# A layer norm's scales: from a chain split between VectorE and GpSimd to a chain on GpSimd alone

## The reference, cut to what matters

```python
def _layernorm(x, axis=-1, eps=1e-05):
    m = jnp.mean(x, axis=axis, keepdims=True)
    v = jnp.var(x, axis=axis, keepdims=True)
    return (x - m) / jnp.sqrt(v + eps)

# x: (4, 1024, 256)
x = x + _layernorm(attn(_layernorm(x)))   # norm 1 inside, norm 2 outside
x = x + _layernorm(ffn(_layernorm(x)))    # norm 3 inside, norm 4 outside
```

## Time and profile before

| what | us |
|---|---|
| median of the 3 timed runs | 1262.3 |
| lowest and highest of them | 1260.84, 1262.65 |
| the profiled execution, its own time | 1258.12 |
| the profiled execution, its span | 1256.3 |
| busy in the span: PE, DVE, POOL, ACT | 1043.6, 705.6, 681.0, 625.3 |

### The profile page before, as it was taken

One profiled execution on the slowest core, in us unless ns is written; L12 is line 12 of the kernel. 1 busy time (PEld: TensorE's weight loads), 2 busy tenths in 40 slices (PEclk: granted clock), 3 DMA queues, 4 the chain that ended last, 5 costly groups with the idle time before them and its releaser, 6 DMA issues. The chain is left out here.

```text
span 1256.3 us, 15452 instructions
## 1 busy us (share of the span) xinstructions
PE 1043.6 (83%) x4736; PEld 832.8 (66%) x4736; DVE 705.6 (56%) x1280; ACT 625.3 (50%) x1190; POOL 681.0 (54%) x605
## 2 busy tenths in 40 slices
PE   4555578887867887797988899969999999999995
PEld 2122265664644655575777688859999999999884
DVE  1699998999988899976796442101111111111045
ACT  3784869778476586668554432212232222232234
POOL 2495967759469786578665347324343433332221
PEclk9676778898887897898999899979999999999998
DMA  5000010202002007113322589359998888887252
GB/s 180 18 28 6 34 34 18 68 1 83 2 1 84 1 18 227 42 22 110 83 96 67 172 236 208 55 150 347 337 316 266 264 276 251 262 273 227 41 176 101
DMA packets 140931, 162.68 MB, mean 129 GB/s; under 512 B 27976, under 2 KB 125984, under 8 KB 140832
## 3 DMA queue, kind: packets, MB, share of 16 engines
q1 hardware_dynamic: 124976, 142.70, 36.0%
q0 software_dynamic: 15872, 18.99, 7.7%
HBM read 135.20 MB, written 26.87 MB: 129 GB/s over the span
## 5 line engine op out<-in xcount | busy, mean ns | idle before, releaser
L1542 POOL TENSOR_TENSOR Ssum<-Ssum,S 128x512 f32<-128x512 f32 x240 | 301.5, 1270 | 105.9 <-DVE S L1162 104.7
L1014 PE MATMUL psum<-w,hT 128*128 128x256 f32 x1152 | 260.0, 384 | 4.2 <-issue 4.2
L1014 PEld LDWEIGHTS psum<-w,hT 128*128 128x128 f32 x1152 | 219.8, 193 | 34.4 <-issue 4.6
L1592 POOL DMA_INDIRECT acc_d<-y,ID x72 | 114.3, 1587 | 236.8 <-DMA acc_d<-y,ID 124.7
L1431 ACT ACTIVATE A<-dts,nea 128x512 f32<-128x512 f32 x256 | 177.3, 720 | 68.6 <-DVE S L1162 40.4
L1470 ACT ACTIVATE hT<-psum,bb 128x256 f32<-128x256 f32 x200 | 83.5, 470 | 244.7 <-PE psum L981 244.7
L981 PE MATMUL psum<-XT,w 128*128 128x256 f32 x800 | 182.8, 386 | 7.4 <-issue 6.5
L1138 DVE TENSOR_TENSOR psum<-us,psum 128x512 f32<-128x512 f32 x256 | 163.4, 682 | 31.6 <-PE psum L902 29.6
L981 PEld LDWEIGHTS psum<-XT,w 128*128 128x128 f32 x800 | 154.0, 194 | 33.9 <-issue 10.7
L1162 DVE TENSOR_TENSOR_SCAN S<-A,carry,psum 128x512 f32<-128x512 f32 x120 | 148.8, 1264 | 0.0
L1296 DVE TENSOR_TENSOR y<-bb,psum 128x256 f32<-128x256 f32 x72 | 27.0, 416 | 209.0 <-PE psum L1014 209.0
(11 more groups left out here) (149 smaller groups left out, 1314.3 us busy)
## 6 DMA issues: line engine op xcount, KB each, us to landing
w<-W SPq DMA_DIRECT2D x94, 1024.0 KB, 6.7
bb<-b SPq DMA_DIRECT2D x47, 128.0 KB, 7.8
xnb<-x SPq DMA_DIRECT2D x16, 256.0 KB, 3.0
Xr<-x SPq DMA_DIRECT2D x16, 256.0 KB, 4.6
x_d<-gb SPq DMA_DIRECT2D x8, 512.0 KB, 2.9
xn_d<-nb SPq DMA_DIRECT2D x8, 512.0 KB, 3.3
X<-x_d SPq DMA_DIRECT2D x16, 256.0 KB, 9.3
ACC<-acc_d SPq DMA_DIRECT2D x16, 256.0 KB, 5.9
```

Source lines behind the costliest of these rows:

```text
L1014: t = eng.matmul(bank(g)[:, 256 * k:256 * k + 256], hT[n % 2][:, f, 128 * k:128 * k + 128], w[:, f, :], start=f == 0, stop=f == 7)
L1542: eng.tensor_tensor(to, to, of, ALU.add).then_inc(nsum, 1)
L1592: eng.indirect_dma_start(acc_d, bass.IndirectOffsetOnAxis(ap=ID[:, col, 1:2].bitcast(u32), axis=0), y[n % NY][:, k, :], None, compute_op=A ...
```

## The change

The step `scales` leaves the plan. VectorE ends its part with the four `bn_aggr`. GpSimd does the rest in the step `stats`: it adds eps to the variance, negates the mean, raises to the power, and multiplies. `mv` gets two buffers per norm, since GpSimd now reads it, and the waits that guard `rs` and `nm` move from VectorE to GpSimd. The next `bn_stats` of VectorE carries a wait for its own last `bn_aggr` (`read`). The small extra chain for 8 edge rows at the start keeps its split.

```diff
@@ finishing
         if i:
             say("normal", 4, i - 1, False)
-        say("scales", 4, i)
@@ buffers
-        mv = {k: put(f"mv{k}", [128, 4, 2]) for k in (1, 2, 3, 4)}
+        mv = {k: [put(f"mv{k}{i}", [128, 4, 2]) for i in range(2)] for k in (1, 2, 3, 4)}
@@ VectorE
-            def scales(kind, i):
-                eng.wait_ge(rstd[kind], i + 1)
-                if i >= 2:
-                    eng.wait_ge(norma[kind], act_normals(kind, i - 2))
-                eng.scalar_tensor_tensor(nm[kind][i % 2], mv[kind][:, :, 0], -1.0, rs[kind][i % 2],
-                                         ALU.mult, ALU.mult).then_inc(nmd[kind], 1)
@@
+                        if j == 0 and read:
+                            eng.wait_ge(*read)
                         i = eng.bn_stats(stats[:, j, :], of(kind, b, j))
                     i.then_inc(statd[kind], 1)
-                    eng.wait_ge(statd[kind], 3 * b + 1)
+                    eng.wait_ge(statd[kind], 2 * b + 1)
+                    if b >= 2:
+                        eng.wait_ge(nmd[kind], b - 1)
                     for j in range(n):
-                        i = eng.bn_aggr(mv[kind][:, j, :], stats[:, j, :])
+                        i = eng.bn_aggr(mv[kind][b % 2][:, j, :], stats[:, j, :])
                     i.then_inc(statd[kind], 1)
-                    eng.wait_ge(statd[kind], 3 * b + 2)
-                    if b >= 2:
-                        eng.wait_ge(norma[kind], act_normals(kind, b - 2))
-                    eng.tensor_scalar(rs[kind][b % 2][:, 0:n], mv[kind][:, 0:n, 1], eps, None,
-                                      ALU.add).then_inc(statd[kind], 1)
+                    read = statd[kind], 2 * b + 2
@@ GpSimd
-                    eng.wait_ge(statd[kind], 3 * b + 3)
-                    eng.tensor_tensor(rs[kind][b % 2][:, 0:n], rs[kind][b % 2][:, 0:n], mhalf[:, 0:n],
-                                      ALU.pow).then_inc(rstd[kind], 1)
+                    r, m = rs[kind][b % 2], nm[kind][b % 2]
+                    eng.wait_ge(statd[kind], 2 * b + 2)
+                    if b >= 2:
+                        eng.wait_ge(norma[kind], act_normals(kind, b - 2))
+                    eng.tensor_scalar(r, mv[kind][b % 2][:, :, 1], 1e-5, None, ALU.add).then_inc(rstd[kind], 1)
+                    eng.tensor_scalar(m, mv[kind][b % 2][:, :, 0], -1.0, None, ALU.mult).then_inc(rstd[kind], 1)
+                    eng.wait_ge(rstd[kind], 3 * b + 1)
+                    eng.tensor_tensor(r, r, mhalf, ALU.pow).then_inc(rstd[kind], 1)
+                    eng.wait_ge(rstd[kind], 3 * b + 3)
+                    eng.tensor_tensor(m, m, r, ALU.mult).then_inc(nmd[kind], 1)
```

More of the change, by code:

```diff
@@ L1042, in apply @@
                                       nm[kind][i % 2][:, j:j + 1], ALU.mult, ALU.add).then_inc(normv[kind], 1)
+            read = None
             done = {}
@@ L1073, in _ @@
                         eng.wait_ge(edge_mv, 1)
-                        eng.bn_aggr(mv[4][0:8, 0, :], stats[0:8, 0, :]).then_inc(edge_mv, 1)
+                        eng.bn_aggr(mv[4][0][0:8, 0, :], stats[0:8, 0, :]).then_inc(edge_mv, 1)
                         eng.wait_ge(edge_mv, 2)
-                        eng.tensor_scalar(rs[4][0][0:8, 0:1], mv[4][0:8, 0, 1:2], eps[0:8], None,
+                        eng.tensor_scalar(rs[4][0][0:8, 0:1], mv[4][0][0:8, 0, 1:2], eps[0:8], None,
                                           ALU.add).then_inc(edge_mv, 1)
@@ L1107, in _ @@
                         eng.wait_ge(edge_mv, 4)
-                        eng.scalar_tensor_tensor(nm[4][0][0:8, 0:1], mv[4][0:8, 0, 0:1], -1.0, rs[4][0][0:8, 0:1],
+                        eng.scalar_tensor_tensor(nm[4][0][0:8, 0:1], mv[4][0][0:8, 0, 0:1], -1.0, rs[4][0][0:8, 0:1],
                                                  ALU.mult, ALU.mult).then_inc(edge_mv, 1)
@@ L1112, in _ @@
                                           ALU.mult, ALU.add).then_inc(edge_n, 1)
[L1113 to L1117, removed]
-                                eng.wait_ge(st_xn, 16 * b)
-                                eng.wait_ge(nT_out, 2 * b)
-                            apply(kind, b)
-                elif step == "scales":
-                    scales(*a)
+                    if both:
+                        if kind == 3:
+                            eng.wait_ge(st_xn, 16 * b)
+                            eng.wait_ge(nT_out, 2 * b)
+                        apply(kind, b)
                 elif step == "dt_sum":
@@ L1486, in _ @@
                     kind, b = a
-                    n = 4
                     if kind == 1 and b == 0:
```

## The result

| | before | changed |
|---|---|---|
| timed, median (range), us | 1262.47 (1260.84 to 1270.02) | 1250.91 (1250.09 to 1254.36) |
| ratio, 95% interval | 1 | 0.9903 (0.9882 to 0.9925) |
| profiled execution, us | 1258.12 | 1254.36 |
| its span, us | 1256.3 | 1252.6 |
| busy: VectorE / GpSimd, us | 705.6 / 681.0 | 684.6 / 704.9 |

The change makes the kernel 11.6 us faster. The forecast was 1246, with 1240 to 1252 as its own range: the sign holds, but of the 16.6 us of the forecast's sum five are missing, and the part of the sum that was to carry most of it is not the part that did.

What follows compares the result with a forecast made beforehand. VectorE bounds the kernel up to 545 us, then TensorE. The terms -3.5 - 13 + 1 - 2.1, less 1 us of gain, give -16.6 us: 1241.5 profiled, 1246 timed; own range 1240 to 1252, whole range 1237 to 1261.

Steps and rivals of the forecast that it cites:

- Before 213 us: From 40 to 213 us, the removed VectorE instructions of 6 chains save 3.5 us, counted in full.
- 213 to 545 us: Second stretch, 12 chains: 20.1 us of VectorE time removed, two thirds (13 us) kept, since VectorE is busy 92%.
- kept in part: Rival: TensorE and ScalarE come last soon after 213 us; a quarter of 20.1 us kept, -9.5 us, 1253; chance 0.22.
- the wrong sign: What would show the forecast wrong: VectorE's waits for residual and TensorE's spreading longer by as much as was removed.
- ScalarE's earlier scales: In 213 to 545 us, nm up to 4 us earlier where ScalarE waits 23.3 and 8.7 us; counted in the upper bound.
- 545 us on, TensorE is the bound: From 545 us TensorE is busy 91.04 of 102 us, so what VectorE is spared there counts as nothing.
- Added on GpSimd: Three small instructions of 0.25 us per chain, 0.85 us with waits; costs 1 us in total, mostly covered by waits.
- The slower rival: GpSimd's backlog: chains at 1.75 us add 24.5 us to the path, +6 us, 1268; chance 0.1 with the last rival.
- The lock in the other direction: Last rival: GpSimd's new instructions stand still behind VectorE's large ones, 1.2 us each; chance 0.1 together with slower.
- The experts equally long: From 730 to 1204 us, the experts only move as a block: they start earlier and nothing in them shrinks.
- The end: Norm 4's last chain: VectorE's last addition starts at 1250.1 instead of 1252.21, -2.1 us.
- The base: Profiled execution of 1258.12 us, with 4.2 us added to reach the timed scale, whose median is 1262.3.

Runs made afterwards that it cites:

- e_two_in: Changed kernel plus, in norms 1 to 3, two unused small VectorE instructions at the old places, with two SBUF inputs or the old scalar form; 0.9928 of before.
- e_one_in: Changed kernel plus, in norms 1 to 3, two unused small VectorE reductions with one SBUF input at the old places; 0.9921 of before.
- e_eps_v: Changed kernel, but in norms 1 to 3 the addition of eps stays on VectorE, with negation, power and product on GpSimd; 0.9935 of before.
- e_prod_v: Changed kernel, but in norms 1 to 3 the product stays on VectorE at its old place, with eps and power on GpSimd; 0.9926 of before.
- e_relay_two: Changed kernel plus two idle two-input VectorE instructions in norms 1 to 3, the second waiting for GpSimd's nm and giving ScalarE its signal; 0.9980 of before.
- e_beside: Changed kernel with fewer expert steps woven into the last three chunks (42 instead of 48), moving two routed groups behind the recurrence; 0.9913 of before.
- e_top2_late: Changed kernel with the router's choice of the second round moved five steps of the plan later; 0.9892 of before.
- e_load: Changed kernel plus four unused small scalar operations on GpSimd behind each chain of norms 1 to 3; 0.9898 of before.

## Why the prediction came out as it did

- **Before 213 us**, 3.5 predicted, 3.8 to 4.0 seen. Right: VectorE has nothing to wait for there.
- **213 to 545 us**, 13 of 20.1 kept predicted. This is the term of the sum that was mis-sized. Between the aggregates at 215 and at 565 us the traces gained 3.5 and 4.0 us. VectorE stood still elsewhere instead: 9.5 us more for TensorE's spreading, 4.7 in the router's longer stall (6.96 instead of 2.25 us), 4.6 for softplus, residual and carry. (These are counted up to a fixed 545 us, where the changed kernel is further on, so they and the 3.5 add up to somewhat more than 20.1.) The premise, that at 92% busy VectorE passes on two thirds, was wrong: a busy share says how often an engine works, not that everybody else has slack when it gets faster. The rival "kept in part" took a quarter, 5 us, and came nearer on this term; the total lies between the two, 1250.9 between 1246 and 1253. What I had named as the wrong sign, longer waits for TensorE's spreading, is what came.
- **The stalls and the hand-off.** The sum was built on the stalls, and counted ScalarE's earlier scales as a small extra inside the upper bound. Neither carries the gain alone. About half of the stalls, with nothing waiting for them, is worth 0.9 to 3.0 us of the 12 (e_two_in against e_one_in and against the changed kernel); all of eps's stalls 2.8 of 11 (e_eps_v); the product's place with ScalarE's full wait 1.7 of 11 (e_prod_v). Stalls together with the dependence are worth 9.6 (e_relay_two). The prediction added the two instructions up line by line, as if each had its own price; the runs show that most of the price belongs to the pair. Through which waits they do this to each other stays open.
- **545 us on, TensorE is the bound**: right, and shown by e_beside. I drew too little from it: it takes back not only what is saved after 545 us but also the lead that VectorE brings along. In e_top2_late a stall of 6.7 us removed at 481 us was worth 2 to 3 at 565 and nothing at the end.
- **Added on GpSimd**: durations right to about 0.05 us; cost of 1 us not to be told from 0 in e_load's time. The slower rival is excluded by e_load, whose chains carry 0.9 us more and which still has the gain.
- **The lock in the other direction** exists (0.24 to 0.74 us, 1.04 to 1.52), in norm 4 only, where VectorE's final additions read two SBUF tiles; that the new instructions would meet no lock held for norms 1 to 3. It costs at most 0.6 us, at the end.
- **The experts equally long**: wrong by about 3 us (492.7 and 493.3 against 490.1), in which TensorE's wait for the gathers has its part.
- **The end**: 2.1 predicted, 1.8 and 2.3 seen.
- **The base.** The sum was made against a profiled execution 4.3 us under the median. The traces once more give 9.2 us, the timed runs 11 to 12; the missing 2 to 3 us are as large as what one execution differs from another, and no trace shows them. That the time falls inside the forecast's own range of 1240 to 1252 owes something to this: by the traces' 9.2 us it would have been 1253.

## What to carry to other kernels

A tiny instruction on a busy engine costs what it waits for and who waits for it, not its 0.15 us: look for its longest duration, and for the engine whose signal it carries. Before adding up what a faster engine saves, list the next waits at the same places and the other engines' instructions that it will now catch up with; the same lock stood 12 us further on. And where two small costs sit in one chain of hand-offs, don't price them one by one: here taking away either brought about three quarters of the gain, and having both cost far more than the sum of the two.

## What the runs showed of the hardware

- A VectorE instruction of 128x64 with two SBUF operands took 6.96 us instead of 0.23, through six of GpSimd's instructions with two SBUF operands, and ended with the last of them. The Trainium skill ("SBUF — State Buffer", section "Who interferes with whom") says that whichever of the two comes second is blocked; the traces agree in both directions (VectorE 0.23 to 6.96 us, GpSimd 0.24 to 0.74 us) and add that the blocked one gets no turn between GpSimd's instructions.
- A reduction of 128x4 at the places of the small instructions was never blocked (at most 0.154 us in 48, of which 15 began inside one of GpSimd's additions, e_one_in).
- GpSimd's scalar operation on 128x4 takes 0.225 to 0.238 us, its product 0.199, its power 1.04. The power lets VectorE by: at 1245.40 an addition from two SBUF tiles, wholly inside the power's 1.04 us, takes its usual 0.69. The other way round, a power that started at 1228.37, just behind such an addition (1228.30), took 1.52. This fits a lock that is held for the reading and writing and not for the time that an instruction takes; no run tests that by itself.
